# Projections, transposes and shift turns of the second attention, split into two 64-row halves

## What is computed

```python
h = _layernorm(x, ln_g, ln_b)
qk, v = jnp.split(h @ W_kv, 2, axis=-1)          # queries and keys are the same
scores = jnp.einsum('bhqd,bhkd->bhqk', qk, qk)
a1 = jax.nn.softmax(scores, axis=-1)
a1 = jnp.einsum('gh,bhqk->bgqk', W_x, a1)        # heads are mixed
o1 = jnp.einsum('bhij,bhjd->bhid', a1, v)
out = o1.transpose(0, 2, 1, 3).reshape(b, n, dims) @ W_out
x = _layernorm(x + out)
```

## Time and profile before

| | |
|---|---|
| median of 3 runs | 1529.43 us (1526.62 to 1534.0) |
| profiled execution | 1530.18 us, span 1527.9 us |
| TensorE busy over the span | 1456.4 us |
| VectorE, ScalarE, GpSimd busy | 1180.8, 1056.9, 967.4 us |
| mean granted TensorE clock | 0.976 of full |

### The profile page before, as it was taken

How to read it: one execution, slowest core, us unless ns; L and a number is a source line. 1 busy time by engine, 2 the same in 40 slices (tenths; PEclk the granted TensorE clock), 3 DMA queues, 4 the chain that set the end, 5 groups by cost and what they waited for, 6 DMA issues and landing times. The chain is left out here.

```text
span 1527.9 us, 55309 instructions
## 1 busy us (share of the span) xinstructions
PE 1456.4 (95%) x17642; PEld 1141.6 (75%) x17642; DVE 1180.8 (77%) x3338; ACT 1056.9 (69%) x2581; POOL 967.4 (63%) x1160
## 2 busy tenths in 40 slices
PE   5999999999999899979999999999999999998998
PEld 3445555554554499959989999999999999897997
DVE  4688888888888478878887888788878887864666
ACT  2477777777778888856777777777777777773332
POOL 4465565656554167777777877787778777852222
PEclk7699999999999999979999999999999999999999
DMA  5345454454444100122222222222222222201211
GB/s 146 105 128 135 132 140 128 132 140 126 134 131 135 34 32 33 55 74 79 82 69 90 76 79 69 90 76 80 69 90 76 80 70 85 75 23 32 65 62 52
DMA packets 174124, 133.93 MB, mean 88 GB/s; under 512 B 13787, under 2 KB 145126, under 8 KB 174054
## 3 DMA queue, kind: packets, MB, share of 16 engines
q1 hardware_dynamic: 172944, 132.37, 30.0%
q10 hardware_dynamic: 1110, 0.66, 0.1%
HBM read 64.82 MB, written 55.05 MB: 78 GB/s over the span
## 5 line engine op out<-in xcount | busy, mean ns | idle before, releaser
L971 DVE TENSOR_REDUCE shifts<-bank 128x2 bf16<-128x512 f32 x1024 | 682.2, 686 | 158.7 <-PE bank L1123 158.1
L912 ACT ACTIVATE probs<-bank 128x512 f32<-128x512 f32 x1024 | 579.9, 595 | 120.1 <-PE bank L1109 116.3
L1071 PE MATMUL bank<-values,probs 64*128 64x129 f32 x8192 | 577.8, 276 | 0.9 <-DVE o_even L938 0.7
L1071 PEld LDWEIGHTS bank<-values,probs 64*128 64x128 f32 x8192 | 528.8, 188 | 20.4 <-issue 4.5
L1123 PE MATMUL bank<-stack 48*128 48x256 bf16 x2048 | 373.3, 277 | 29.7 <-DVE shifts L971 24.1
L1109 PE MATMUL bank<-stack 49*128 49x256 bf16 x2048 | 373.3, 274 | 7.6 <-ACT probs L912 2.4
L715 POOL TENSOR_TENSOR values<-mix,v_in 128x1024 f32<-128x1024 f32 x128 | 302.3, 2363 | 0.0
L1109 PEld LDWEIGHTS bank<-stack 49*128 49x128 bf16 x2048 | 163.9, 95 | 139.4 <-ACT probs L912 89.7
L724 POOL TENSOR_TENSOR o_odd<-o_odd,scaled 128x256 f32<-128x256 f32 x224 | 163.5, 730 | 128.0 <-ACT scaled L838 124.3
L838 ACT ACTIVATE scaled<-bank,recips 128x128 f32<-128x128 f32 x448 | 138.6, 360 | 92.8 <-DVE recips L965 92.7
L1123 PEld LDWEIGHTS bank<-stack 48*128 48x128 bf16 x2048 | 156.2, 96 | 54.0 <-DVE shifts L971 37.8
(11 more groups left out here) (165 smaller groups left out, 2176.8 us busy)
## 6 DMA issues: line engine op xcount, KB each, us to landing
stack<-score_parts SPq DMA_DIRECT2D x64, 512.0 KB, 4.2
stack<-score_parts SPq DMA_DIRECT2D x256, 96.0 KB
score_parts<-parts SPq DMA_DIRECT2D x256, 64.0 KB, 2.1
score_parts<-parts SPq DMA_DIRECT2D x128, 96.0 KB, 2.6
score_parts<-parts SPq DMA_DIRECT2D x64, 192.0 KB, 2.3
x_in_f<-x_all SPq DMA_DIRECT2D x64, 128.0 KB, 2.0
score_parts<-parts SPq DMA_DIRECT2D x64, 128.0 KB, 2.2
x_in<-in_L_attn_x SPq DMA_DIRECT2D x32, 128.0 KB, 2.1
```

The costliest lines, as they stand in the source:

```text
L912: act.activation(probs[:, s % RING, :, :].rearrange("p t n -> p (t n)"), s2[s % 2][:, :], ACT.Exp, scale=scale).then_inc(exp_done, 1)
L971: dve.tensor_reduce(shifts[:, :, hf, col], s1_bank(s)[:, :].rearrange("p (t n) -> p t n", t=TILES), op=ALU.max, axis=AX.X, negate=True).th ...
L1071: return pe.matmul(pv_bank(h)[:, q * (D + 1):(q + 1) * (D + 1)], probs[rows, h % RING, t, q * P:(q + 1) * P], values[b.odd][rows, t, h, :] ...
```

## The change

In the steps in which items i and i + 1 both exist, slots 1, 9, 11 and 13 of the second attention get an order of their own, `rows_with_others`. Each projection and turn becomes two matmuls, one over rows 0 to 63 and one over rows 64 to 127, both into the same place of `m1`. The projections' halves accumulate. The turns, which were transposes, become matmuls with the identity: each half takes 64 rows of the source as weights and 64 columns of the identity, and writes 64 columns. The halves on the lower tile stand at the beginning of the slot, those on the upper tile at its end; the upper ones follow a wait of TensorE for a score that it issued itself (`lower_half_is_done`). The semaphores `shifts_in_psum`, `qk_in_psum`, `ot_in_psum`, `out_in_psum`, `v_in_psum` and `xt_in_psum` are raised by the last half. Shifts of the second attention are turned into fp32 values at columns `TOK` on, and ScalarE reads them there. The orders of the other engines are not changed.

```diff
--- before.py
+++ after.py
@@ -817,7 +817,8 @@
             act.wait_ge(shifts_in_psum, b.number() * 2 + (hf + 1))
 
             wait(act, shifted[hf], b.number() * 16)
-            act.activation(shift_rows[hf][:, :], m0[:, :].bitcast(BF16)[0:half_heads, SHIFTS_AT:SHIFTS_AT + TOK], ACT.Copy).then_inc(shift_rows_ready, 1)
+            turned_shifts = m0[:, :].bitcast(BF16)[0:half_heads, SHIFTS_AT:SHIFTS_AT + TOK] if first else m0[0:half_heads, TOK:2 * TOK]
+            act.activation(shift_rows[hf][:, :], turned_shifts, ACT.Copy).then_inc(shift_rows_ready, 1)
...
@@ -1040,9 +1041,40 @@
             pe.wait_ge(max_done, b.number() * HEADS + half_heads * (hf + 1))
             for t in range(TILES):
                 to = SHIFTS_AT + t * P
-                last = pe.transpose(m0[:, :].bitcast(BF16)[0:half_heads if first else P, to:to + P], shifts[:, t, hf, :],
-                                    core.ident_bf[:, :])
+                if first:
+                    last = pe.transpose(m0[:, :].bitcast(BF16)[0:half_heads, to:to + P], shifts[:, t, hf, :], core.ident_bf[:, :])
+                else:
+                    last = pe.matmul(m0[:, TOK + t * P:TOK + (t + 1) * P], shifts[:, t, hf, :], core.ident_bf[:, :],
+                                     start=True, stop=True)
             last.then_inc(shifts_in_psum, 1)
+
+        def shifts_half_turned(b, hf, half, t):
+
+            if half == 0 and t == 0:
+                pe.wait_ge(max_done, b.number() * HEADS + half_heads * (hf + 1))
+            rows = slice(half * TILE_ROWS, (half + 1) * TILE_ROWS)
+            to = TOK + t * P + half * TILE_ROWS
+            turn = pe.matmul(m0[:, to:to + TILE_ROWS], shifts[rows, t, hf, :], core.ident_bf[rows, rows], start=True, stop=True)
+            if half == 1 and t == TILES - 1:
+                turn.then_inc(shifts_in_psum, 1)
+
+        def half_turned(at, source, half, t):
+
+            rows = slice(half * TILE_ROWS, (half + 1) * TILE_ROWS)
+            to = at + t * P + half * TILE_ROWS
+            return pe.matmul(m1[:, to:to + TILE_ROWS], source[rows, t, :], core.ident[rows, rows], start=True, stop=True)
+
+        def half_projected(at, left, right, half, t):
+
+            rows = slice(half * TILE_ROWS, (half + 1) * TILE_ROWS)
+            return pe.matmul(m1[:, at + t * P:at + (t + 1) * P], left[rows, t * P:(t + 1) * P], right[rows, :],
+                             start=(half == 0 and t == 0), stop=(half == 1), skip_group_check=True)
+
+        def q_half_projected(b, half):
+
+            rows = slice(half * TILE_ROWS, (half + 1) * TILE_ROWS)
+            return pe.matmul(m1[:, 0:TOK], core.w1_qk[rows, :], x_t[b.odd][rows, :], start=(half == 0), stop=(half == 1),
+                             skip_group_check=True)
 
...
+
+        def rows_with_others(i, on, s):
+
+            def lower(k):
+                if on(0 if s >= 2 else -1):
+                    lower_product(i if s >= 2 else i.plus(-1), (s - 2) % HEADS, k)
+
+            def upper(k):
+                if on(0 if s >= 3 else -1):
+                    upper_product(i if s >= 3 else i.plus(-1), (s - 3) % HEADS, k)
+
+            def lower_score(t):
+                first_score(i.plus(1), s, t)
+
+            def upper_score(t):
+                second_score(i, s, t)
+
+            def lower_half_is_done():
+                pe.wait_ge(max_in_psum, i.plus(1).number() * HEADS + (s + 1))
+
+            if s == slots.shifts1:
+                pe.wait_ge(shift_rows_ready, i.number() * 2 + 1)
+                wait(pe, v_taken, times(i, 1, n))
+                wait(pe, xt_ready, times(i, 2, n))
+                shifts_half_turned(i, 1, 0, 0)
+                upper_score(0)
+                shifts_half_turned(i, 1, 0, 1)
+                upper_score(1)
+                if on(slots.q_ahead):
+                    q_half_projected(i.plus(slots.q_ahead), 0)
+                upper(0)
+                upper(1)
+                lower_score(0)
+                upper(2)
+                lower_score(1)
+                lower(0)
+                upper(3)
+                lower(1)
+                lower_half_is_done()
+                if on(slots.q_ahead):
+                    q_half_projected(i.plus(slots.q_ahead), 1).then_inc(qk_in_psum, 1)
+                lower(2)
+                shifts_half_turned(i, 1, 1, 0)
+                lower(3)
+                shifts_half_turned(i, 1, 1, 1)
+            if s == slots.ot:
+                wait(pe, part0_ready, times(i, 2, n))
+                wait(pe, shift_rows_ready, times(i, 0, n) * 2)
+                wait(pe, v_taken, times(i, 1, n))
+                wait(pe, y_ready, times(i, -2, n))
+                pe.wait_ge(pv_taken, (i.number() * half_heads + (BESIDE // 2 + 1)) * TILES)
+                shifts_half_turned(i.plus(1), 0, 0, 0)
+                upper_score(0)
+                shifts_half_turned(i.plus(1), 0, 0, 1)
+                upper_score(1)
+                if on(-1):
+                    pe.wait_ge(o_ready, times(i, -1, n))
+                    half_turned(0, o, 0, 0)
+                upper(0)
+                if on(-1):
+                    half_turned(0, o, 0, 1)
+                upper(1)
+                lower_score(0)
+                upper(2)
+                lower_score(1)
+                lower(0)
+                upper(3)
+                lower(1)
+                lower_half_is_done()
+                shifts_half_turned(i.plus(1), 0, 1, 0)
+                shifts_half_turned(i.plus(1), 0, 1, 1)
+                lower(2)
+                if on(-1):
+                    half_turned(0, o, 1, 0)
+                lower(3)
+                if on(-1):
+                    half_turned(0, o, 1, 1).then_inc(ot_in_psum, 1)
...
+            if s == slots.v:
+                wait(pe, y_ready, times(i, -1, n))
+                wait(pe, part0_ready, times(i, 2, n))
+                pe.wait_ge(shift_rows_ready, i.plus(1).number() * 2 + 1)
+                if on(3):
+                    pe.wait_ge(x_loaded[i.plus(3).odd], (i.plus(3).half + 1) * 16)
+                    half_turned(0, x_in[i.plus(3).odd], 0, 0)
+                upper_score(0)
+                if on(3):
+                    half_turned(0, x_in[i.plus(3).odd], 0, 1)
+                upper_score(1)
+                if on(slots.v_ahead):
+                    pe.wait_ge(xt_ready, times(i, slots.v_ahead, n))
+                    half_projected(TOK, x_t[i.plus(slots.v_ahead).odd], core.w1_kv[:, 1, :], 0, 0)
+                upper(0)
+                if on(slots.v_ahead):
+                    half_projected(TOK, x_t[i.plus(slots.v_ahead).odd], core.w1_kv[:, 1, :], 0, 1)
+                upper(1)
+                lower_score(0)
+                upper(2)
+                lower_score(1)
+                lower(0)
+                upper(3)
+                lower(1)
+                lower_half_is_done()
+                if on(slots.v_ahead):
+                    half_projected(TOK, x_t[i.plus(slots.v_ahead).odd], core.w1_kv[:, 1, :], 1, 0)
+                lower(2)
+                if on(slots.v_ahead):
+                    half_projected(TOK, x_t[i.plus(slots.v_ahead).odd], core.w1_kv[:, 1, :], 1, 1).then_inc(v_in_psum, 1)
+                lower(3)
+                if on(3):
+                    half_turned(0, x_in[i.plus(3).odd], 1, 0)
+                    half_turned(0, x_in[i.plus(3).odd], 1, 1).then_inc(xt_in_psum, 1)
...
 
@@ -1286,6 +1453,9 @@
 
         def step(i, on):
             for s in range(HEADS):
+                if not first and on(0) and on(1) and s in (slots.shifts1, slots.ot, slots.out, slots.v):
+                    rows_with_others(i, on, s)
+                    continue
                 if first:
                     others_of_first(i, on, s)
                 else:
```

More of the change, by code:

```diff
@@ L1134, in both_scores @@
                     first_score(i.plus(1), s, t)
+        def rows_with_others(i, on, s):
[68 more added lines that the diff above has]
+                    half_turned(0, o, 1, 1).then_inc(ot_in_psum, 1)
+            if s == slots.out:
+                if on(-1):
+                    pe.wait_ge(ot_ready, times(i, -1, n))
+                    pe.wait_ge(shift_rows_ready, i.plus(1).number() * 2 + 1)
+                    half_projected(0, o_t, core.w1_out, 0, 0)
+                upper_score(0)
+                upper_score(1)
+                if on(-1):
+                    half_projected(0, o_t, core.w1_out, 0, 1)
+                upper(0)
[7 more added lines that the diff above has]
+                lower(2)
+                if on(-1):
+                    lower_half_is_done()
+                    half_projected(0, o_t, core.w1_out, 1, 0)
+                lower(3)
+                if on(-1):
+                    half_projected(0, o_t, core.w1_out, 1, 1).then_inc(out_in_psum, 1)
+            if s == slots.v:
+                wait(pe, y_ready, times(i, -1, n))
+                wait(pe, part0_ready, times(i, 2, n))
```

(31 more changed lines are left out.)

## The result

The changed kernel takes 1589.94 us (median of 4 runs, 1588.36 to 1591.48) against 1528.81 us before (4 runs, 1526.62 to 1534.0). The ratio is 1.0395, with a 95% interval of 1.0372 to 1.0418: 61 us slower. I had forecast 1571, between 1548 and 1592.

The account below looks back on a forecast made before the run. TensorE, 95% busy, was taken to bound the kernel. 74 us lost to two ScalarE holds less 32 us gained on TensorE gave +42 us on the profiled 1530.18 us, roundly 1571 us, range 1548 to 1592.

Parts of the forecast that it names:

- dear turns or a lower clock: Half turns in slots 9 and 13 take 0.38 us each, or TensorE's granted clock drops; 1591 us, chance 0.12.
- The gain on TensorE: Split slots without drains shorten TensorE's step from 21.76 to 20.7 us: 1.03 a step, 32 us over 31 steps.
- laid out: TensorE slot times forecast by adding streams per tile: slot 9 1.67 us, slot 11 1.56, slot 13 2.22, slot 1 1.78.
- small hold: Before the change, slots 8 and 0 each had 0.15 us of hold; slot 8's would stay, slot 0's would go.
- The holds: Products of slots 10 and 14 wait for ScalarE's scaling behind late copies: 1.27 and 1.23 us, 74 us lost in all.
- The half turns: Half turns of o and x_in in slots 9 and 13 taken at 0.22 us each, range 0.11 to 0.38.
- cheap: Rival: half turns go at streaming speed, 0.22 us less in each of slots 9 and 13; 1557 us, chance 0.10.
- a slot no shorter than before: Sign of being wrong: slots 1, 9 and 11 no shorter than before would mean that the halves don't overlap.
- no overlap: Rival: halves don't run beside the other tile's work, 2.8 us of extras a step paid twice; 1657 us, chance 0.05.
- one hold only: Rival: products stand still in only one of slots 10 and 14; 1534 us, no difference, chance 0.05.
- the hold does not bite: Rival: ScalarE's scaling of heads 5 and 9 is still in time, TensorE's gain is left; 1498 us, chance 0.08.
- The waits that I covered at nothing: Other moved signals, such as y's wait for the out projection, forecast to cost nothing; holds in slots 12 or 2 would refute.

Follow-up runs that it names:

- the first experiment: Against the changed kernel: ScalarE's copies of o_t, of slot 9's shift rows and of x_t moved one slot later, behind scaling and exp; 1539.92 us.
- the fourth: Against the changed kernel: only the copies of o_t and of the shift rows one slot later, x_t staying in slot 13; 1583.45 us, ratio 1.0322.

## Why the prediction was right, and what was mis-sized

**The bound and the mechanism held.** ScalarE's scaling of heads 5 and 9 stands behind copies that wait for the last instruction of the slot; that takes more than TensorE gains. It is shown in three ways: the 60 waits, their disappearance when the copies move (a step from 23.8 to 21.11 us), and one hold each in the runs of slot 9 and slot 13 alone, which came within 2 us of what this theory, with the holds as read in the changed kernel, gave for them (1569.5 against 1568, 1561.4 against 1561).

**The number owes something to luck.** 1590 lies 2 us inside the range, and the range reached so far only for the rival of dear turns or a lower clock, which gave 1591. That rival's conditions did not come. What made up the difference from 1571 are several small terms, all on one side.

**The gain on TensorE was over-sized.** The term "TensorE alone would gain 21.76 - 20.7 = 1.03 us a step" measures 0.65 (21.76 - 21.11 in the first experiment). Slots 1 and 11 came out as laid out, 1.78 and 1.56 us. The printed sum has two slips that matter little: slot 9's terms give 1.65, not 1.67, and 21.76 - 20.7 is 1.06; 1.03 comes of the unrounded 20.73. Four places took longer than laid out. Slot 9 takes 1.76 us (1026.54 to 1028.30) instead of 1.67. Slot 13 takes 2.29 (1033.47 to 1035.76) instead of 2.22. Slots 2 to 8 take 8.10 (1018.44 to 1026.54) instead of 7.95. And slot 0 is free of its small hold only in the changed kernel (1.14 us), where VectorE catches up during the large ones; with these gone, in the first experiment, it takes 1.29 (1033.81 to 1035.10), so that 0.15 was counted as gained and was not. That it is VectorE's lag which decides slots 8 and 0 I argue; no run tested it. The two traces agree for slot 0: VectorE's reciprocals for head 11 start at 1038.39 in the changed kernel, after 1.30 us of idle, and at 1032.95 in the first experiment, without any, straight behind its reduction.

**The holds were a little under-sized.** "1.27" and "1.23" were 2.50 us a step; the step with them less the step without is 2.7 on average. Slots 10 and 14 take 2.49 (1028.30 to 1030.79) and 2.39 us (1035.76 to 1038.15), in the first experiment 1.13 and 1.06. From the copy to the products the intervals are those read before, and the wait up to the copy was right within 0.1: the last half turn of `o` starts 0.37 us ahead of `o_t`.

By these terms a full step was forecast at 20.7 + 2.5 = 23.2 us and takes 23.8; 0.6 x 31 = 18 of the 19 us between 1571 and 1590.

**The half turns cost what I took.** Their records start 0.11 us apart (1028.07, 1028.18). That is what loading gives, 0.10 to 0.11; streaming 64 columns would be half a score's 0.11, 0.06. So the rivals of cheap and of dear turns are out. It is also why slot 9 gains nothing by the split: two transposes of 128 columns took 0.33 us before (1020.78 to the scores at 1021.11), and their halves hold each tile for 4 x 0.11 = 0.44. One of the signs that I had named for being wrong, a slot no shorter than before, so came true for slot 9, though the halves do overlap: it takes 1.76 us, and took 1.57 before (1020.66 to 1022.23, drain ahead of it not counted). Slot 13, with two half turns on each tile beside its v projection, takes 2.29 after 1.98 (1026.66 to 1028.64). The lines of before are

```profile
1022.23 0.27 PE L1123 MATMUL bank<-stack 48*128 48x256 bf16 x1
1025.35 0.27 PE L1123 MATMUL bank<-stack 48*128 48x256 bf16 x1
1028.64 0.27 PE L1123 MATMUL bank<-stack 48*128 48x256 bf16 x1
```

With slots 8 and 12, whose drains the split removes, it is 3.17 for slots 8 and 9 after 3.03 (from 1019.20), and 3.41 for slots 12 and 13 after 3.29 (from 1025.35), of which slot 14 gives 0.12 back (1.18 us before, 1.06 in the first experiment).

**Of the other rivals**, no overlap is out (slot 11 takes 1.56 us where plain slot and out projection, one behind the other, took 1.77: 1023.58 to 1025.35), the clock is full, one hold only is what the runs of single slots look like, and "the hold does not bite" came true only when ScalarE's order was changed with it: 1507.5 in the first experiment without its long steps, where 1498 was given, and by the second attention alone 1529 - 18 = 1511.

**The waits that I covered at nothing cost nothing**: VectorE waits for the out projection (`y`, 0.4 us at most), no product waits for it, and slot 12 takes 1.12 us (1032.35 to 1033.47), a plain slot's time.

**Not tried:** to raise the turn's signal early inside the slot. All the halves write the one bank that ScalarE would then read, and the Trainium skill ("PSUM — Partial Sum Buffer", Terms) says that two engines at work on the same bank and the same quadrant of 32 partitions at once are an error; no run here shows what would happen.

## What to carry to other kernels

When work is spread out over a slot so that an engine never drains, its completion signal moves to the end of the slot. Before making the change, go to the engine that waits for that signal and read what stands behind the wait in its queue. If something there is needed sooner than the signal, move the waiting instruction behind it in the same change; alone that move is worth nothing (1.000), with the split it is worth 3 to 5%. And count a half of a small matmul by its weight load: splitting the transposes of slot 9 gained nothing, splitting the projections of slots 1 and 11 did.

## What the runs showed of the hardware

The long steps of the first experiment. In this stretch of its profiled execution TensorE and GpSimd are at rest for 3.3 us at the head of TensorE's loop, and VectorE and ScalarE have 0.2 to 0.3 us of work left. TensorE then runs at the lower of its two clock levels from 852 to 858 us (granted clock 0.50; over the last stretch below 0.56 on average):

```profile
840.00:848.00 8.00, 7.25 (x127) 7.06 (x122) 6.62 (x23) 5.67 (x16) 7.51 (x10) 1.00 0.20 57
848.00:851.30 3.30, 0.00 (x0) 0.00 (x0) 0.22 (x1) 0.30 (x1) 0.00 (x0) 1.00 0.32 104
851.30:859.00 7.70, 6.42 (x57) 5.84 (x59) 2.32 (x7) 1.96 (x5) 0.72 (x1) 0.56 0.08 25
```

The same place in TensorE's order of time. Nothing that the profile shows released it ("issue"); the branch that closes the loop stands at 846.40:

```profile
851.34 0.28 PE L1141 MATMUL bank<-stack 49*128 49x256 bf16 x1 [4.09 <-issue]
```

And the instruction queue of the page, for this kernel and for the changed one:

```profile
q8 instruction: 69, 1.13, 0.3%
```

```profile
q8 instruction: 41, 0.67, 0.2%
```

So some 28 packets of 16 KB were fetched in addition, about 9 for each of the three long steps. In the trace those of this step start between 847.0 and 891.4 us, two at the loop's head and seven over the pass that follows. The step is 8.5 us longer: 4.1 us of rest at the loop's head, the rest a second pause of 1.24 us within the next 3 us, and the half clock. The Trainium skill ("Runtime: NRT & Kernel Launch", Instruction fetch mechanics) says that instructions come in blocks of 16 KiB and that a taken branch whose target lies outside the current window of two such pages waits for a fetch. The trace agrees with the packet size and with the place, the loop's head. By that rule alone every pass would pay, though, for the loop is longer than two packets (seven more follow in one pass); here every third to fifth pass paid in the first experiment and every second in the fourth, and the others nothing. The runs narrow it: the same loop 64 or 128 instructions further on did not pay it, longer loops did not, and the changed kernel did not, with the same instructions on TensorE in the same place. For each of these it is read from one profiled execution; the others of the same kernel (4, 4, 10, 6 and 4 runs in all) lie within 4, 4, 7, 6 and 3 us of each other, less than one long step. Only the two kernels with all four slots split and the copies of slot 9 moved did. So neither length nor TensorE's program alone decides; place and timing are left, and which of them, and how, stays open.
